# Attention scores as full-precision matmuls on halves of the array's rows, with 6 key tiles turned on TensorE and 10 over DRAM

## The reference

```
h = layernorm(x)                                  # 2048 x 128
c_q = h @ w_down_q.T; c_kv = h @ w_down_kv.T      # 2048 x 64 each
q = (c_q @ w_up_q.T) as 16 heads of 64; k, v likewise from c_kv
q, k = rope(q), rope(k)                           # e*cos - o*sin, e*sin + o*cos over all 64
scores = q @ k^T / 8                              # 16 x 2048 x 2048
out = softmax(scores) @ v                         # 2048 x 1024
x = x + (out @ w_out.T + x)                       # then layer norm
```

## Time and profile before

| | |
|---|---|
| median of three runs | 2464.31 us |
| the profiled execution's own time | 2464.99 us |
| its span | 2462.8 us |
| TensorE matmul busy | 2126.8 us, 86% |
| VectorE busy | 1676.6 us, 68% |
| ScalarE busy | 1381.8 us, 56% |
| GpSimd busy | 897.5 us, 36% |
| scores on TensorE, 2056 records | 561.7 us busy |
| transposes on TensorE, 2048 records | 321.4 us busy |
| mixing on TensorE, 1056 + 1056 records | 257.4 + 255.2 us busy |
| mean granted TensorE clock | 0.934 |

### The profile page before, as it was taken

How to read it: one execution, slowest core, us unless ns; L and a number is a source line. 1 busy time by engine, 2 the same in 40 slices (tenths; PEclk the granted TensorE clock), 3 DMA queues, 4 the chain that set the end, 5 groups by cost and what they waited for, 6 DMA issues and landing times. The chain is left out here.

```text
span 2462.8 us, 38107 instructions
## 1 busy us (share of the span) xinstructions
PE 2126.8 (86%) x11662; PEld 1309.8 (53%) x11662; DVE 1676.6 (68%) x3033; ACT 1381.8 (56%) x2802; POOL 897.5 (36%) x883
## 2 busy tenths in 40 slices
PE   4745699877984599999999999999999999997397
PEld 2532377435862255556555555555565555553244
DVE  5767766596666477777677777677776777774544
ACT  4233465255630277777677777677776777774121
POOL 0625543264420344443334434344443444433000
PEclk8878899898997699999999999999999999998598
DMA  1001000000001467776677767667776677764100
GB/s 31 1 1 57 1 2 12 20 1 1 2 12 48 154 220 230 239 240 228 215 227 234 247 225 238 211 229 242 233 234 222 222 235 239 232 231 146 36 1 18
DMA packets 224395, 345.61 MB, mean 140 GB/s; under 512 B 16993, under 2 KB 169697, under 8 KB 223905
## 3 DMA queue, kind: packets, MB, share of 16 engines
q1 hardware_dynamic: 224160, 342.86, 42.1%
HBM read 148.55 MB, written 136.31 MB: 116 GB/s over the span
## 5 line engine op out<-in xcount | busy, mean ns | idle before, releaser
L1479 DVE TENSOR_REDUCE g.most<-g_score 128x1 f32<-128x512 f32 x1028 | 639.3, 683 | 342.3 <-PE g_score L1449 341.8
L1487 ACT ACTIVATE g.probs<-g_score,g.bias 128x1024 f32<-128x1024 f32 x514 | 568.0, 1110 | 65.1 <-DVE g.bias L1482 53.7
L1449 PE MATMUL g_score<-g.keys,g.q_unit 128*128 128x512 f32 x2056 | 561.7, 413 | 25.8 <-DMA g.q_unit<-g.q_pair 11.9
L1472 ACT ACTIVATE g.near<-g_turned 128x512 f32<-128x512 f32 x512 | 305.2, 596 | 325.9 <-PE g_turned L1468 325.7
L1449 PEld LDWEIGHTS g_score<-g.keys,g.q_unit 128*128 128x128 f32 x2056 | 361.3, 190 | 145.6 <-ACT g.probs L1487 60.1
L1468 PEld LDWEIGHTS g_turned<-top.ident,g.probs 128*128 128x128 f32 x2048 | 234.1, 140 | 243.2 <-issue 208.1
L1546 DVE STREAM_TRANSPOSE g.blocks<-g.probs 128x1024 f32<-128x1024 f32 x256 | 318.9, 1246 | 31.4 <-DMA bounce<-g.blocks 16.1
L1468 PE MATMUL g_turned<-top.ident,g.probs 128*128 128x128 f32 x2048 | 321.4, 279 | 0.0
L1500 PE MATMUL g_mix_ps<-g.near,mid.y_tok 128*64 128x512 f32 x1056 | 257.4, 609 | 6.3 <-DMA g.far<-bounce 6.3
L1500 PE MATMUL g_mix_ps<-g.far,mid.y_tok 128*64 128x512 f32 x1056 | 255.2, 605 | 0.0
L1566 POOL TENSOR_TENSOR mid.y_tok<-mid.y_tok,g.waves 128x512 f32<-128x512 f32 x128 | 163.7, 1279 | 229.7 <-ACT mid.y_tok L1464 229.7
(11 more groups left out here) (358 smaller groups left out, 3235.6 us busy)
## 6 DMA issues: line engine op xcount, KB each, us to landing
bounce<-g.blocks SPq DMA_DIRECT2D x256, 512.0 KB, 5.2
g.far<-bounce SPq DMA_DIRECT2D x256, 512.0 KB, 4.4
g.q_unit<-g.q_pair SPq DMA_DIRECT2D x132, 256.0 KB, 4.4
g.keys<-g.k_part SPq DMA_DIRECT2D x256, 64.0 KB, 3.5
g.far<-g.near SPq DMA_DIRECT2D x8, 512.0 KB, 5.5
lt.turns<-turns SPq DMA_DIRECT2D x1, 2048.0 KB, 8.1
g.waves<-g_waves SPq DMA_DIRECT2D x1, 2048.0 KB, 10.2
g.keys<-g.probs SPq DMA_DIRECT2D x16, 128.0 KB, 2.4
```

The source lines that it names most:

```text
L1449: ins = nc.tensor.matmul(score[:, b], q[:, part], k_of(b), start=(part == 0), stop=(part == 1))
L1472: nc.scalar.activation(near[:, w, tiles, r * P:(r + 1) * P], turned[:].rearrange("p (t n) -> p t n", n=P), ACT.Copy).then_inc(m["near_copi ...
L1479: nc.vector.tensor_reduce(most[:, slot, k:k + 1], score[:, k], AX.X, ALU.max, negate=True)\
L1487: nc.scalar.activation(probs[:, slot, k * 2 * CH:(k + 1) * 2 * CH], score[:, 2 * k:2 * k + 2].rearrange("p b n -> p (b n)"), ACT.Exp, bias ...
```

## The change

The type F32R and the split into parts go. `keys` and `queries` are plain 32-bit floats, 64 rows per head; keys of even and odd blocks of 512 lie on the lower and the upper 64 partitions, queries on both. A bank is one full-precision matmul over 64 rows (two records), and the two banks of a pair are on opposite halves of the rows (`score_pair`). `row_max` takes a maximum over two banks at once. `make_parts` adds straight into place: two adds for keys, four for queries (each head on both halves); `queries` holds the whole pair of heads, so nothing is moved by DMA any more (`send_keys`, `send_q` and their semaphores go). One semaphore, `parts_ready`, counts the finished parts. 6 key tiles are turned on TensorE, three at a time, and 10 go over DRAM. There are four block buffers and four `written` semaphores, one for each r, and each read back is issued behind the write of the next row tile. The mixing in rows with r = 0 now touches two tiles that come over DRAM, so its wait for them moves from r = 1 to r = 0. Ahead of the loop the same is done in larger steps: VectorE places keys, GpSimd places queries.

```
-NEAR = 8
+NEAR = 6
+TURN = NEAR // 2
...
-        keys = sp.sb("keys", [P, 2, 2, S], F32R)
-        q_pair = sp.sb("q_pair", [P, 2, S], F32R)
-        q_unit = sp.sb("q_unit", [P, 2, 2, QW], F32R)
+        keys = sp.sb("keys", [P, 2, 2, S // 2])
+        queries = sp.sb("queries", [P, 2, 2, S])
         w_up = sp.sb("w_up", [P, 2, 2 * P])
-        k_part = sp.sb("k_part", [P, 2, QH], F32R)
         probs = sp.sb("probs", [P, 2, S])
         near = sp.sb("near", [P, 2, NEAR, QW])
         far = sp.sb("far", [P, 2, RT * 4, FAR, 32])
-        blocks = sp.sb("blocks", [P, 2, 4, FAR, 32])
-        most = sp.sb("most", [P, 2, 4])
+        blocks = sp.sb("blocks", [P, RT, 4, FAR, 32])
+        most = sp.sb("most", [P, 2, 2])
...
+        def place_keys(engine, turn, head, at, width, first, second):
+
+            block, inside = divmod(at * width, CH)
+            cols = slice(block // 2 * CH + inside, block // 2 * CH + inside + width)
+            return engine.tensor_tensor(keys[block % 2 * 64:block % 2 * 64 + 64, turn, head, cols],
+                                        first[head * 64:head * 64 + 64], second[head * 64:head * 64 + 64], ALU.add)
+        def place_queries(engine, turn, head, half, at, width, first, second):
+
+            return engine.tensor_tensor(queries[half * 64:half * 64 + 64, turn, head, at * width:(at + 1) * width],
+                                        first[head * 64:head * 64 + 64], second[head * 64:head * 64 + 64], ALU.add)
...
                 nc.gpsimd.memset(near[:], 0.0).then_inc(m["zeroed"], 1)
-                for n in range(PIECES):
-                    pool.wait_ge(m["first_free"], 2 * n + 2)
-                    nc.gpsimd.tensor_tensor(cos_part[:, n % 2], cos_part[:, n % 2], sin_part[:, n % 2], ALU.add)\
-                        .then_inc(m["roped"], 1)
-                nc.gpsimd.memset(zero[:], 0.0)
+                for c_ in range(NC):
+                    pool.wait_ge(m["first_free"], 4 * c_ + 4)
+                    for crossed in range(2):
+                        pool.wait_ge(m["zeroed"], 1 + 4 * c_ + 2 * crossed)
+                        for head in range(2):
+                            place_queries(nc.gpsimd, 0, head, head ^ crossed, c_, CH, cos_part[:, 1], sin_part[:, 1])\
+                                .then_inc(m["zeroed"], 1)
+                    pool.wait_ge(m["zeroed"], 5 + 4 * c_)
+                    pool.sem_inc(m["q_first"], 1)
...
+                    if kind == 0:
+                        dve.wait_ge(m["first_free"], 2 * n + 2)
+                        for head in range(2):
+                            ins = place_keys(nc.vector, 0, head, c_, CH, cos_part[:, 0], sin_part[:, 0])
+                        ins.then_inc(m["k_first"], 1)
...
-        def score_banks(pe, banks, q, k_of):
-
-            for b in banks:
-                for part in range(2):
-                    ins = nc.tensor.matmul(score[:, b], q[:, part], k_of(b), start=(part == 0), stop=(part == 1))
-                ins.then_inc(m["score_done"], 1)
+
+        def score_pair(pe, pair, turn, head, chunk, r):
+
+            cols = slice(chunk * QW + r * P, chunk * QW + (r + 1) * P)
+            for odd in range(2):
+                rows = slice(odd * 64, odd * 64 + 64)
+                nc.tensor.matmul(score[:, 2 * pair + odd], queries[rows, turn, head, cols],
+                                 keys[rows, turn, head, pair * CH:(pair + 1) * CH], start=True, stop=True)\
+                    .then_inc(m["score_done"], 1)
...
         def row_max(dve, slot, before):
 
-            for k in range(4):
-                dve.wait_ge(m["score_done"], 4 * before + k + 1)
-                nc.vector.tensor_reduce(most[:, slot, k:k + 1], score[:, k], AX.X, ALU.max, negate=True)\
-                    .then_inc(m["maxes"], 1)
-            dve.wait_ge(m["maxes"], 4 * before + 4)
+            for k in range(2):
+                dve.wait_ge(m["score_done"], 4 * before + 2 * k + 2)
+                nc.vector.tensor_reduce(most[:, slot, k:k + 1], score[:, 2 * k:2 * k + 2].rearrange("p b n -> p (b n)"),
+                                        AX.X, ALU.max, negate=True).then_inc(m["maxes"], 1)
+            dve.wait_ge(m["maxes"], 2 * before + 2)
             nc.vector.tensor_reduce(bias[:, slot:slot + 1], most[:, slot], AX.X, ALU.min).then_inc(m["bias_ready"], 1)
...
         def turn_blocks(dve, r, G):
 
             dve.wait_ge(m["exp_done"], 2 * G + 2)
-            dve.wait_ge(written[r % 2], 8 * (G - r % 2) + 16)
-            nc.vector.transpose(blocks[:, r % 2].rearrange("p j t c -> p t j c"),
+            dve.wait_ge(written[r], 4 * (G - r) + 16)
+            nc.vector.transpose(blocks[:, r].rearrange("p j t c -> p t j c"),
                                 probs[:, r % 2, NEAR * P:].rearrange("p (t j a) -> p t j a", j=4, a=32))\
                 .then_inc(m["blocks_turned"], 1)
 
         def write_blocks(sync, w, r, G):
             sync.wait_ge(m["blocks_turned"], G + 2)
             sync.dma_start(bounce[4 * w + r].rearrange("(p x) -> p x", p=P),
-                           blocks[:, r % 2].rearrange("p j t c -> p (j t c)")).then_inc(written[r % 2], 16)
+                           blocks[:, r].rearrange("p j t c -> p (j t c)")).then_inc(written[r], 16)
 
         def read_blocks(sync, w, r, G):
-            sync.wait_ge(written[r % 2], 8 * (G - r % 2) + 32)
+            sync.wait_ge(written[r], 4 * (G - r) + 32)
             sync.dma_start(far[:, w, 4 * r:4 * r + 4].rearrange("p i t c -> p i (t c)"),
                            bounce[4 * w + r].rearrange("(i p x) -> p i x", i=4, p=P)).then_inc(landed[w], 16)
-        def make_parts(pool, g, j, at, half, kind):
-
-            n = 3 * (2 * half + kind)
+        def make_parts(pool, turn, at, half, kind):
+
             both = raw[:, kind]
-            total = both[:, 0:QH]
+            first, second = both[:, 0:QH], both[:, QH:]
+            n = 8 * half + 3 * kind
             pool.wait_ge(m["piece_taken"], 2 * half + 2 + kind)
             nc.gpsimd.tensor_tensor(both, both, waves[:, at].rearrange("p s n -> p (s n)"), ALU.mult)\
                 .then_inc(m["order"], 1)
             pool.wait_ge(m["order"], n + 1)
-            nc.gpsimd.tensor_tensor(total, total, both[:, QH:], ALU.add).then_inc(m["order"], 1)
-            pool.wait_ge(m["order"], n + 2)
             if kind == 0:
-                high, low = k_part[:, 0], k_part[:, 1]
-                pool.wait_ge(m["k_loaded"], 256 + 64 * half)
+                for head in range(2):
+                    place_keys(nc.gpsimd, turn, head, at, QH, first, second).then_inc(m["order"], 1)
+                    pool.wait_ge(m["order"], n + 2 + head)
             else:
-                high, low = (q_pair[:, part, at * QH:(at + 1) * QH] for part in range(2))
-                pool.wait_ge(q_loaded[1], 32 * (4 * g + j + 1))
-            nc.gpsimd.tensor_tensor(high, total, zero[:].broadcast_to([P, QH]), ALU.add).then_inc(m["order"], 1)
-            pool.wait_ge(m["order"], n + 3)
-            nc.gpsimd.tensor_tensor(low, total, high.bitcast(F32), ALU.subtract).then_inc(m["low_ready"], 1)
-            pool.wait_ge(m["low_ready"], PIECES + 2 * half + 1 + kind)
-            pool.sem_inc(m["raw_free"], 1)
+                for crossed in range(2):
+                    for head in range(2):
+                        place_queries(nc.gpsimd, turn, head, head ^ crossed, at, QH, first, second)\
+                            .then_inc(m["order"], 1)
+                    pool.wait_ge(m["order"], n + 3 + 2 * crossed)
+            pool.sem_inc(m["parts_ready"], 1)
...
                                 write_blocks(sync, w, 0, G)
-                                if w == 1:
-                                    send_keys(sync, 1 - turn, 2 * j + 1, H + 1)
+                                read_blocks(sync, 1 - w, 3, G - 1)
                                 write_blocks(sync, w, 1, G + 1)
                                 sync.wait_ge(m["mix_done"], U + 1)
                                 read_blocks(sync, w, 0, G)
-                                read_blocks(sync, w, 1, G + 1)
                                 if j == 0 and w == 0:
                                     sync.wait_ge(m["piece_full"], 2 * H + 2)
                                     load_w(sync, turn, g + 2)
                                 write_blocks(sync, w, 2, G + 2)
+                                read_blocks(sync, w, 1, G + 1)
+                                write_blocks(sync, w, 3, G + 3)
                                 read_blocks(sync, w, 2, G + 2)
-                                write_blocks(sync, w, 3, G + 3)
-                                if w == 0:
-                                    send_keys(sync, 1 - turn, 2 * j, H)
-                                sync.wait_ge(m["score_done"], 16 * U + 16)
-                                send_q(sync, w, (j + 1) % NC)
-                                read_blocks(sync, w, 3, G + 3)
```

(44 more changed lines are left out.)

92 lines of the change are left out of this document (29 added, 63 removed).

## The result

The changed kernel took 2476.57 us (median of six runs, 2470.85 to 2478.24), the kernel before on the same chip 2467.19 (six runs, 2462.95 to 2468.85): a ratio of 1.0036, 95% interval 1.0024 to 1.0048, or +9.4 us. The direction is the forecast one, and the time lies in the stated range (2446 to 2512) and in that of the likeliest case; the size is not: +25 was forecast. The two profiled executions differ by 6.0 in span (2468.8 against 2462.8); the changed kernel's was the fastest of its six.

The account below looks back on a forecast made before the run. TensorE is full (42.91 us per eight rows), and in short rows the circle through the score banks binds equally. 10 + 13 + 6 - 5 + 1 = +25 on 2464.99 gave 2490, stated as 2488; range 2446 to 2512.

Parts of the forecast that it names:

- the likeliest case: The forecast itself: +25 us, stated as 2488 us, with 2470 to 2508 as its own range; chance 0.47.
- the rows: Eight row tiles of the loop: 43.22 us against 42.91, +0.31, times 32 = +10 us (bounds -29 and +60).
- the first scores: Before the loop: first scores start near 840 instead of 845.59, -5 us (-10 to 0).
- Transposes: TensorE: two of eight fewer per row, 0.10 to 0.11 us each; new groups of three take 0.39 to 0.48.
- seams: TensorE's switches between full-array and half-array work, twice per short row instead of once: 0.17 and 0.06 us more.
- scores: TensorE: eight records on 64 rows, paired on opposite halves, take 1.89 us, 0.05 less than now (1.75 to 3.4).
- circle: Short rows, from scores through maxima and exponentials to the next scores in the banks: 5.00 us, 0.26 longer (4.90 to 5.30).
- Rival 1: TensorE's tiling switches are free and the transposes' gain reaches the end: rows -29 us, 2445 in all; chance 0.21.
- GpSimd is late at a pair's end: TensorE waits 1.6 us for the last query part before row (1,3)'s scores, once in 32 rows: x 8 = +13.
- The lock on the reciprocals, +6: Rows (1,3): VectorE's small add before its maxima is held while GpSimd adds, 0.2 us on 28 rows, +6 (0 to 13).
- The last write and read are longer: +1: After the loop: the last block write and read back over DRAM take longer, +1 us.
- DMA: cost 0: Loop transfers: 640 KB blocks instead of 512, 243 GB/s, four block buffers let a write take four rows; cost 0.

## Why the prediction was right in direction and wrong in size

The sum was +25, and the profiled executions differ by +6.0. Of the 19 between them, 6 are the reciprocals, 5.8 the end, 3.4 the rows, 1.2 the first scores and the rest turns and remainder.

- **Transposes, seams, scores, circle**: right. The groups and the circle's sum came within 0.05 us (inside the circle VectorE's first maximum came at 1.20 instead of 1.12). The rows came to +6.6 instead of +10, because two seams that I carried over from today's projections vanish when the scores are half-array too. Rival 1 fell: it wanted groups of three of 0.30, 0.42 and 0.33, and they take 0.47, 0.48 and 0.38.
- **GpSimd is late at a pair's end**: right in place and length. But +13 was a gross price. Taken away, it gave 3.2 back in the profiled executions (9.2 by the medians), because three of the eight idles stand right ahead of a turn and the last ahead of the end, where something else is late next. I had asked that question for stalls that go, not for one that comes.
- **The lock on the reciprocals, +6: the step that failed outright.** The add is held 0.58, as forecast, and in all 32 rows (1,3), but in these rows VectorE waits for scores behind it, 0.34 or more: measured 0. I had added the delay without its slack. In rows (0,3), where the add takes 0.12, VectorE waits 0.80 for scores: that is the slack. (Its "28 rows" are 24, too: 32 less the eight with the wait for GpSimd.)
- **"The last write and read are longer: +1": wrong in size and in sign, and the second step that failed.** From the last scores to the end the profiled executions take 225.6 in the kernel before, 222.0 with the new order, 225.8 with order and tiles, 224.6 with the new scores as well but without the wait for GpSimd, and 220.8 in the changed kernel. So the order gave 3.6, the longer transfers cost 3.8 rather than 1, and most of the fall to 220.8 is the last wait for GpSimd, behind which the transfers catch up. I sized the transfers, and neither their place in the queue nor what stands ahead of them. A step of 1 to 3 us here is within what two like kernels differ by (223.5 with two buffers).
- **"DMA: cost 0"**: right for the changed kernel, for the wrong reason, and so luck. The cover that I named, four buffers, did nothing; the order did all. With the old order the same blocks cost 59. And the order alone gives the kernel before 11.7, which the earlier trace rows do not show, because I read VectorE's busy time and not its wait for writes.

By ratios to the kernel before: order 0.9960, tiles on top 0.9878, new scores on top of both 1.0026. The change consists of two gains of some 29 us together and one loss of 36. The loss is the circle and the seams, 1.42 us in eight rows (43.11 against 41.69), x 32 = 45, and the waits for GpSimd's parts, 13, less what turns (12), start (7) and end (5) give back in the profiled executions; the two parts of the 45 were not taken apart in full, but the four short rows alone hold 1.14 of the 1.42. What the new scores do buy, the DMA room, pays only with 12 tiles over DRAM, and even then (2440.92) no more than equals old scores with 10 (2438.39; the intervals of the two ratios overlap).

## What to carry to other kernels

When a change is a bundle, forecast each part against the kernel before, and ask of each whether it needs another: tiles without the order cost 7%, with it they gain 0.8%. A delay on an engine counts only beyond the idle that stands behind it, and an idle counts only beyond what is late next; both need the row that follows, not only the one that is delayed. In one in-order queue, an instruction that waits for a landing holds all behind it: put what waits one place later.

## Hardware behaviour that I had not expected

- Of a write and a read of 640 KB that one queue issues half a microsecond apart, the first lands sooner: read first, the read lands in 4.9 us and the write in 6.6; write first, the write in 3.9 and the read in 6.0.
- No seam between two groups of matmuls that both use half of the rows: the scores follow the projections after 0.96, where the full-array scores followed after 1.07. The Trainium skill (TensorEngine Tiling, Key Properties) ties the drain to a change of mode, which agrees: here there is none.
- The turn of the loop costs TensorE an idle with no releaser (3.1 to 4.1 us in the changed kernel, 4.7 to 6.1 with old scores and 10 tiles). Behind it the granted clock is 0.50 for some microseconds, and what runs there takes nearly twice as long (scores 3.52 instead of 1.92). Together that is 15 us in three turns of the changed kernel, 21 without the wait for GpSimd, 27 with old scores and 10 tiles. No run took the idle apart.
- With 12 tiles over DRAM and the old scores' copies the 16 DMA engines were full at 329 GB/s (share 0.98 over 280 us).
